# In the third layer the sync queue issues relation types, target rows and the mask ahead of the sources four chunks on

## The reference

```python
x = _layernorm(x + _L0_gnn_ref(x, edge_index, edge_weight, edge_attr_64, ...))   # attention over edges
x = _layernorm(x + _L1_gnn_ref(x, src, dst, L1_gnn_W1, ...))                     # mean of sources, two products
x = _layernorm(x + _L2_gnn_ref(x, L2_gnn_weight, src, dst, edge_type_8))         # one matrix per relation
x = _layernorm(x + _L3_gnn_ref(x, ..., src, dst, edge_type_3, node_type_3))      # matrices per edge and node type
```

```python
hw = jnp.einsum('ni,rio->nro', h, weight)
msg = hw[src, rel]
out = jax.ops.segment_sum(msg, dst, num_segments=n_nodes)
```

## Time and profile before

| | us |
|---|---|
| median of 3 runs | 1772.02 (1771.62 to 1773.1) |
| the profiled execution's own time | 1771.28 |
| its span, first to last instruction | 1769.5 |
| PE busy | 1434.3 (81%) |
| DVE busy | 1420.3 (80%) |
| POOL busy | 1235.5 (70%) |
| ACT busy | 1111.9 (63%) |

### The profile page before, as it was taken

How to read it: one execution, slowest core, us unless ns; L and a number is a source line. 1 busy time by engine, 2 the same in 40 slices (tenths; PEclk the granted TensorE clock), 3 DMA queues, 4 the chain that set the end, 5 groups by cost and what they waited for, 6 DMA issues and landing times.

```text
span 1769.5 us, 22899 instructions
## 1 busy us (share of the span) xinstructions
PE 1434.3 (81%) x6078; PEld 919.2 (52%) x6078; DVE 1420.3 (80%) x3056; ACT 1111.9 (63%) x2769; POOL 1235.5 (70%) x910
## 2 busy tenths in 40 slices
PE   4788888888888487777758788788789699999995
PEld 2555555555555376666645444444445355555552
DVE  5898998999898599999977676775777577788874
ACT  1677887888787768888884555455556434443342
POOL 7888888777778787778755554544544558888874
PEclk8888888888888799999988988888889899999998
DMA  7444444534443556777652433434324433344320
GB/s 167 97 101 106 107 113 112 110 98 108 97 110 77 130 144 183 184 185 191 181 142 73 142 96 109 132 97 127 108 86 129 128 83 93 95 101 102 92 78 22
DMA packets 165797, 205.06 MB, mean 116 GB/s; under 512 B 66825, under 2 KB 97920, under 8 KB 165668
## 3 DMA queue, kind: packets, MB, share of 16 engines
q1 hardware_dynamic: 108068, 179.45, 36.5%
q0 software_dynamic: 57600, 24.15, 8.2%
HBM read 147.12 MB, written 70.80 MB: 123 GB/s over the span
## 4 chain that ended last, share of the span: by engine, by line
PE 44%; DVE 20%; ACT 18%; issue 7%; DMA 6%; POOL 4%; SPq 1%; POOLq 0%; DVEq 0%; ACTq 0%
PE po L1368 20%; PE pb L1603 7%; DMA rel<-in_etype 5%; DVE bst L754 5%; PE pt L1357 4%; ACT x L1066 4%; DVE run L829 3%; POOL slot_all L532 3%; PE pc L1477 2%; ACT so L1262 2%; ACT res L1066 2%; PE po L1363 2%; ACT do L1066 2%; ACT xt L1109 2%; ACT so L1066 2%
## 5 line engine op out<-in xcount | busy, mean ns | idle before, releaser
L532 POOL DMA_INDIRECT xs<-target_rows,slot_all x236 | 315.0, 1335 | 234.4 <-DMA xs<-source_rows 157.9
L1066 ACT ACTIVATE x<-y,nmr,rst 125x128 f32<-125x128 f32 x800 | 322.6, 484 | 100.3 <-DVE nmr L779 100.3
L1368 PE MATMUL po<-wnt,rt 128*125 128x384 f32 x800 | 299.5, 521 | 0.0
L1357 PE MATMUL pt<-ident,x 125*128 125x125 f32 x800 | 130.7, 289 | 112.4 <-issue 112.4
L1368 PEld LDWEIGHTS po<-wnt,rt 128*125 128x125 f32 x800 | 163.3, 207 | 98.2 <-issue 23.4
L964 DVE SCALAR_TENSOR_TENSOR masked<-rel,st 128x500 f32<-128x500 int32 x175 | 107.0, 671 | 121.3 <-DMA rel<-in_etype 104.1
L1368 PE MATMUL po<-wnt,run 128*125 128x384 f32 x600 | 201.5, 486 | 0.0
L539 POOL DMA_INDIRECT out_rows<-do,last_all x100 | 146.6, 1466 | 65.4 <-issue 44.7
L1357 PEld LDWEIGHTS pt<-ident,x 125*128 125x128 f32 x800 | 100.3, 153 | 149.4 <-issue 147.9
L1603 PE MATMUL pb<-masked,wr 128*128 128x500 f32 x350 | 167.7, 623 | 0.0
L1066 ACT ACTIVATE do<-yd,nmr,rst 125x128 f32<-125x128 f32 x400 | 163.7, 483 | 6.2 <-DVE nmr L779 6.2
(11 more groups left out here) (190 smaller groups left out, 3100.8 us busy)
## 6 DMA issues: line engine op xcount, KB each, us to landing
xin<-in_x SPq DMA_DIRECT2D x100, 224.0 KB
out_rows<-res SPq DMA_DIRECT2D x100, 224.0 KB
source_rows<-so SPq DMA_DIRECT2D x75, 224.0 KB
target_rows<-do SPq DMA_DIRECT2D x75, 224.0 KB
xs<-source_rows SPq DMA_DIRECT2D x59, 224.0 KB
same<-same_d SPq DMA_DIRECT2D x50, 250.0 KB, 4.6
rel<-in_etype SPq DMA_DIRECT2D x50, 250.0 KB, 4.8
xd<-target_rows SPq DMA_DIRECT2D x46, 224.0 KB
```

Source lines behind the costliest of these rows:

```text
L532: return nc.gpsimd.indirect_dma_start(out=to, out_offset=None, in_=table, in_offset=bass.IndirectOffsetOnAxis(ap=index, axis=0), bounds_ch ...
L1066: last = A(to[:, j, :], y[:, j, :], ACT.Identity, scale=rst[s][:, k:k + 1], bias=nmr[s][:, k:k + 1])
L1357: last = nc.tensor.transpose(tile_of(to, j), rows_[:, j, :], ident[0:R, 0:R])
L1368: last = mm(po[0:R, j * 512:j * 512 + NT * D], left(j), wnt[:, k, :, :].rearrange("k t d -> k (t d)"), start=start, stop=stop, skip_group_ ...
```

## The change

In SP's loop of the third layer the call `sources2(c + 4)` moves from ahead of `relations2(c + 2)` to behind `sums2(c + 2)`. No instruction is added or removed, and all waits stay as they are.

```diff
                 d = block_of(2, c)
                 if d + 3 < NC:
                     load_dense(d + 3)
-                if there(c + 4):
-                    sources2(c + 4)
                 if there(c + 2):
                     relations2(c + 2)
                 if there(c + 1):
                     targets2(c + 1)
                 if there(c + 2):
                     sums2(c + 2)
+                if there(c + 4):
+                    sources2(c + 4)
                 if c == EC - 1:
                     sources3(0)
                     targets3(0)
```

## The result

| | before | after |
|---|---|---|
| median, us | 1771.82 (4 runs, 1768.39 to 1773.1) | 1664.49 (4 runs, 1663.26 to 1665.43) |
| the profiled execution's own time, its span | 1771.28, 1769.5 | 1664.54, 1662.7 |
| ratio | | 0.9397, 95% interval 0.938 to 0.9413 |

The change made the kernel 6.0% faster; 1664.7 us was forecast.

The account below looks back on a forecast made before the run. DVE's wait for `rel`, held in SP's queue behind the wait for `so`, was taken as the bound. 13.6 + 20 x 13.3 = 279.6 us instead of 386.9 gave 1664.7 us, range 1656 to 1701.

Parts of the forecast that it names:

- step 1: SP's queue: `rel` issued about 1 us after the next scan, 4.1 to 5.3 us to spare; DVE's wait goes.
- step 2: Third layer, scan to scan: with the wait gone, DVE's chain sets the period at 13.3 us.
- The three chains: Ways from scan to scan: DVE 13.2 us, PE and ACT 13.0 us, PE alone 12.7 us.
- step 3: First shortened period, from the scan of chunk 1: 13.6 us, as `so` and the roots stay where they were.
- step 4: SP's queue: `sources2` behind `sums2` still leaves right behind `so`, at T (scan start) + 10.3 us; cost 0.
- step 5: POOL's gathers of source rows: ready 7 us or more before PE turns them; cost 0, the nearest cover.
- step 6: DMA engines: the same 7.2 us of transfers a chunk in 13.3 us, share 0.54; effect taken as 0.
- step 7: PE's clock: full 2.4 GHz level with 0.6 us of idle time a chunk, already counted in the period.
- The rival of a clock that keeps falling: PE's short idle time loses the full clock in each chunk: period 15.04 us, 1700.9 us in all; chance 0.09.
- POOL: Rival: POOL's seven instructions a chunk each grow by 0.4 us, so POOL sets 14.7 us periods: 1692.7 us; chance 0.06.
- The sum: Third layer, scans of chunks 1 to 22: 279.6 us instead of 386.9, 107.3 us less.

Follow-up runs that it names:

- `rel` alone: Changed kernel with only the `rel` load ahead of the sources, target rows and mask behind them again: 1667.3 us, ratio 0.9387.
- the third buffer: Kernel before in its old order, with three buffers for `rel` and its load one chunk sooner: 1667.3 us, ratio 0.9377.
- less DVE work: Changed kernel without the two statistics instructions of `sel` in the third layer's loop: 1664.4 us, ratio 0.9341.
- sooner roots: Changed kernel with ACT's first roots ahead of the `res` copies, nothing left out: 1658.6 us, ratio 0.9359; timed again 1657.6 us, 0.9347.
- `rel` last: Changed kernel with the `rel` load moved behind target rows, mask and sources: 1749.3 us, ratio 0.9853.
- PE kept busy: Kernel before with five unread matmuls added on PE in each chunk of the third layer: 1749.2 us, ratio 0.9813.
- three ahead, last: Changed kernel with sources loaded three chunks ahead instead of four, still behind `rel`, target rows and mask: 1695.5 us, ratio 0.9555.

## Why the prediction was right

- *The wait goes in full* (step 1): yes. `rel` leaves 0.87 us after the scan, where about 1 was worked out. The experiments with `rel` alone and with the third buffer show that its lateness was the whole cause.
- *What is late next* (step 2): 13.3 us was taken, 13.12 measured. The three chains were ranked wrongly, though it cost only 20 x 0.18 = 3.6 us. DVE was put at 13.2 and is 13.05: I had counted to the end of the variances and added a hand-over, but the masks start 0.09 before that end (1107.57 against 1107.49 + 0.17), so it is 11.14 + 1.92 = 13.06. The way through PE and ACT was put at 13.0 and is 13.12: 11.04 from the transposes to the last root (1097.74 to 1108.78) in place of 10.93, which came from a chunk in which the transposes took 0.60 and not 0.70 us. With 1.31 ahead and 0.76 behind, that is the whole period. It is this chain that bounds the kernel after, by 0.07 us: less DVE work changed nothing, sooner roots did. PE alone is 12.54, not 12.7: the last matmul's modelled end overlaps the next one's start.
- *The first of them* (step 3): 13.63 measured, 13.6 said.
- *The moved load costs nothing* (step 4): it leaves at 1092.28, right behind `so`, and SP waits at line 375 as before. `so` itself ends some 9 us after its scan (1083.30), not 10.3; the full clock, taken in step 7, was not carried to here.
- *The gathers* (step 5): covered, by more than 5 us. The durations were those of a quiet queue: where the change leaves the load it takes 4.0 us, near the 3.7 counted (1092.28 to a gather at 1096.25, for which POOL waited 1.90 us), but 5.1 to 7.4 in or behind a burst. `so`'s wait happens to place the load in the quiet part of the chunk. The cost of nothing doesn't hang on that: four chunks ahead, the load may go into the burst as well.
- *DMA* (step 6): the share was to be 0.54 and is 0.58 over the stretch from chunk 1 to 22 and 0.60 from 1000 to 1200 us, so the transfers of a chunk took 7.6 us (0.58 of 13.16), not 7.2. That landings could be shorter when spread was named without a size; the run with `rel` last shows 1.3 us.
- *The clock* (step 7): 1.00 with 0.3 us of idle time a chunk. The rival of a clock that keeps falling did not occur, and with it the Trainium skill's reading ("TensorE: Matmul & The Clock Gate", "A second HAM failure mode: psum-queue depth-cycling"), by which idle times that are short but frequent enough, between groups of matmuls, make the gate swing: here twenty idle times of 0.3 us in a row left it at the upper level. Of the 0.6 us that the prediction had to expect, the kernel before with PE kept busy has the nearest case: PE idles 7.9 of the 200 us there, some 0.7 us in each of twelve chunks, and its clock is 1.00 as well. What the clock had cost before, 1.85 us a period, was not worked out in the prediction, only contained in it.
- *POOL*: its seven instructions did not stretch beside a DVE that is 98% busy: 142.71 us for 107 in 200 us is 1.33 each, where they were 1.37. The port lock that the Trainium skill describes ("SBUF — State Buffer", "SBUF: two separate sides") cost nothing that can be seen here; whether these instructions take the lock at all, no run tells.
- *The sum*: 107.3 us less was said. It is 110.5 in the stretch, and 3.7 were given back ahead of the scan of chunk 1 and behind that of chunk 22, of which the prediction had nothing; 1.9 of them stand before the changed loop begins, and the cause of the rest is open. The errors of 3.2 and 3.7 cancel, so the hit to 0.2 us is luck; the mechanism's own error is 3%.

## What to carry to other kernels

In a queue that issues in program order, look at what stands behind the wait that is longest, and ask for each DMA there whether it needs that wait; either an issue moved ahead or one buffer more cures it. When such a stall goes, work out the length of each remaining chain from scan to scan, since the gain ends at the longest, and take durations of DMAs from the moment at which they will run, in the burst or outside it. A stall that idles PE costs a second time through the clock, so the gain of removing it is larger than the wait.

## What the runs showed of the hardware

- A load of 224 KB took 3.7 to 4.0 us from issue to its reader with nothing issued shortly ahead of it (before, after), and 7.4 us behind five transfers of 224 to 250 KB each (three ahead, last).
- DMAs issued behind a load delayed it as well: `rel` took 3.86 us to its reader (median to landing 3.4) with only stores behind it, the first 0.7 us later, and 5.15 us (median 4.8) with target rows and mask right behind.
- Matmuls whose results nobody reads, in the time in which PE waited, held the granted clock at 1.00 where it was 0.87, and made the kernel before 1.9% faster (0.9794 to 0.9831).
